# Splitting the first loads of a TensorE-bound LSTM and sign-weight FFN kernel into smaller pieces on two DMA queues

## The reference

```python
xW = einsum('ntd,dg->ntg', x, Wx) + b            # x (32, 64, 256), Wx (256, 1024)
for t in range(64):                               # LSTM, h and c (32, 256), h0 = cond
    a = xW[:, t] + h @ Wh                         # Wh (256, 1024)
    i, f, o, g = sigmoid(a0), sigmoid(a1), sigmoid(a2), tanh(a3)
    c = f * c + i * g
    h = o * tanh(c)                               # hs[:, t] = h
w0, w1, w2 = where(k0, 1, -1), where(k1, 1, -1), where(k2, 1, -1)
u = 2 * relu(s0 * (concat(hs, -hs) @ w0))         # 1024 features
u = 2 * relu(s1 * (u @ w1))                       # 1024
y = x + s2 * (u @ w2)                             # 256
```

## Time and profile before

| what | us |
|---|---|
| median of three runs | 278.2 |
| lowest and highest of them | 277.32 and 278.24 |
| the profiled execution, its own time | 277.77 |
| its span (first to last instruction) | 276.0 |
| TensorE busy in the span | 272.2 |

### The profile page before, as it was taken

The page is one execution under the profiler, slowest core; times in us unless marked ns, Lnnn a source line. Parts: engine busy times, 40 slices in busy tenths (PEclk is TensorE's granted clock), DMA queues, the critical chain, the costliest instruction groups (busy, mean ns, idle before and its releaser), DMA issues.

```text
span 276.0 us, 8792 instructions
## 1 busy us (share of the span) xinstructions
PE 272.2 (99%) x3616; PEld 224.0 (81%) x3616; DVE 203.5 (74%) x751; ACT 158.0 (57%) x482; POOL 2.2 (1%) x10
## 2 busy tenths in 40 slices
PE   8999999999999999999999999999999999999996
PEld 5887888888999998999999999999999996444443
DVE  3778888878888888888888888888887876532213
ACT  5689787878566656655555566555665554411100
POOL 0200000000000000000000000000000000000000
DMA  6970000000000000000000000000000000010002
GB/s 221 362 298 1 4 2 0 2 4 2 2 2 0 5 21 21 2 2 4 21 23 2 1 21 21 2 2 23 22 3 0 21 23 2 0 38 2 0 0 76
DMA packets 5191, 8.72 MB, mean 32 GB/s; under 512 B 672, under 2 KB 3488, under 8 KB 5024
## 3 DMA queue, kind: packets, MB, share of 16 engines
q1 hardware_dynamic: 4864, 7.64, 7.8%
q10 hardware_dynamic: 288, 0.52, 0.5%
HBM read 6.07 MB, written 2.10 MB: 30 GB/s over the span
## 4 chain that ended last, share of the span: by engine, by line
PE 97%; DMA 1%; DVE 0%; DVEq 0%; issue 0%
PE WK L465 50%; PE WK L448 14%; PE G L427 11%; PE ACC L481 10%; PE G L418 9%; DMA x<-in_x 1%; PE G L448 1%; PE ACC L448 1%; PE G L481 0%; DVE xs L715 0%; DVE x L662 0%; DVEq L237 0%
## 5 line engine op out<-in xcount | busy, mean ns | idle before, releaser
L465 PE MATMUL WK<-h,k 128*128 128x256 f16 (+1 forms) x992 | 124.2, 276 | 0.0
L465 PEld LDWEIGHTS WK<-h,k 128*128 128x128 fp8e5 x992 | 94.2, 98 | 13.4
L609 ACT ACTIVATE tT<-aT 128x128 f32<-128x128 f32 x126 | 39.0, 310 | 56.4 <-DVE aT L759 55.2
L655 DVE SCALAR_TENSOR_TENSOR h<-WK,h 128x256 f16<-128x256 f32 (+1 forms) x105 | 42.6, 439 | 24.7 <-ACT h L574 24.7
L759 DVE TENSOR_REDUCE aT<-G 128x128 f32<-128x256 f32 x128 | 48.1, 417 | 7.7 <-PE G L427 6.1
L574 ACT ACTIVATE h<-WK 128x256 f16<-128x256 f32 (+1 forms) x104 | 36.3, 387 | 28.8 <-PE WK L465 28.8
L556 ACT ACTIVATE G<-xw 128x256 f32<-128x256 f32 x126 | 46.6, 370 | 0.0
L448 PE MATMUL WK<-xs,wxs 128*128 128x512 f32 x168 | 42.5, 400 | 0.0
L427 PE MATMUL G<-h,w 128*128 128x64 f16 x1008 | 39.5, 192 | 0.0
L418 PEld LDWEIGHTS G<-h,w 128*128 128x128 f16 x1008 | 32.9, 96 | 5.8 <-DVE h L776 4.4
L448 PEld LDWEIGHTS WK<-xs,wxs 128*128 128x128 f32 x168 | 30.4, 188 | 5.9
(11 more groups left out here) (66 smaller groups left out, 132.8 us busy)
## 6 DMA issues: line engine op xcount, KB each, us to landing
x<-in_x SPq DMA_DIRECT2D x3, 512.0 KB, 7.8
out_y<-x SPq DMA_DIRECT2D x12, 128.0 KB, 1.8
xw<-in_wh SPq DMA_DIRECT2D x4, 256.0 KB, 4.8
k<-in_k SPq DMA_DIRECT2D x1, 1024.0 KB, 9.6
x<-in_x ACTq DMA_DIRECT2D x2, 256.0 KB, 3.8
xw<-in_wx SPq DMA_DIRECT2D x4, 128.0 KB, 3.9
xw<-in_wx SPq DMA_DIRECT2D x2, 256.0 KB, 5.1
k<-in_k SPq DMA_DIRECT2D x1, 512.0 KB, 6.9
```

The source lines that it names most:

```text
L465: ins = eng.matmul(layer_src(tile), w, rhs, start=a == 0, stop=last)
L609: eng.activation(tT[:, B * j0:B * j1], aT[:, j0:j1].rearrange("p j b -> p (j b)"), ACT.Tanh, scale=half_gain0 if t == 0 else half_gain).th ...
L655: eng.scalar_tensor_tensor(layer_dst(tile, 1), layer_src(tile), 0.0, layer_dst(tile, 0), ALU.max, ALU.subtract).then_inc(lo_made[tile[0]])
```

## The change

Wx's first piece (k=0, gate tiles 0-1, 128 KB) becomes two of 64 KB, one for each gate tile, so there are seven pieces. x's quarter 0, half k=0 is loaded in two DMAs of 128 KB: columns 0 to 255 by ACT's queue and columns 256 to 511 by SP's, behind the first piece of Wx. Its high part is made in two casts, the first columns by DVE and the last by ACT (`xh0_end`), and TensorE and `x_lo(0, 0)` wait for both. x's half k=1 moves from ACT's queue to SP's, behind Wx's third piece. In the first matmuls the order of (tile, a) changes so that tile 1's low-weight matmul comes after two more of tile 0's. `wx_hi` and `wx_lo` of the pieces are renumbered. Nothing is computed that was not computed before.

```diff
-WX_GROUPS = ((0, 1, 0, 2), (0, 1, 2, 4), (1, 2, 0, 2), (1, 2, 2, 4), (0, 2, 4, 6), (0, 2, 6, 8))
+WX_GROUPS = ((0, 1, 0, 1), (0, 1, 1, 2), (0, 1, 2, 4), (1, 2, 0, 2), (1, 2, 2, 4), (0, 2, 4, 6), (0, 2, 6, 8))
...
         def wait_x_hi(e, i, k):
             if i == 0 and k == 0:
                 e.wait_ge(xh0, 1)
+                e.wait_ge(xh0_end, 1)
...
-            for g in range(4):
-                load_wx(g)
+            load_wx(0)
+            eng.dma_start(x[:, 0, 0, 256:512], x_d[:, 0, 0, 256:512]).then_inc(dx0_end, 16)
+            load_wx(1)
+            load_wx(2)
+            eng.dma_start(x[:, 0, 1], x_d[:, 0, 1]).then_inc(dx0[1], 16)
+            load_wx(3)
+            load_wx(4)
             eng.dma_start(small[:, :], small_d[:, :]).then_inc(dsmall, 16)
             for g in range(4):
                 eng.dma_start(wh[:, 2 * g:2 * g + 2], wh_d[:, 2 * g:2 * g + 2]).then_inc(dwh[g], 16)
                 if g == 0:
-                    load_wx(4)
-            load_wx(5)
+                    load_wx(5)
+            load_wx(6)
...
             for a0 in (0, 3):
                 for j0 in (0, 2):
-                    for a in range(a0, a0 + 3):
-                        for j in (j0, j0 + 1):
-                            matmul(("x", 0, j), a)
+                    for j, a in ((0, 0), (1, 0), (0, 1), (0, 2), (1, 1), (1, 2)):
+                        matmul(("x", 0, j0 + j), a0 + a)
...
-            eng.dma_start(x[:, 0, 0], x_d[:, 0, 0]).then_inc(dx0[0], 16)
-            eng.dma_start(x[:, 0, 1], x_d[:, 0, 1]).then_inc(dx0[1], 16)
+            eng.dma_start(x[:, 0, 0, 0:256], x_d[:, 0, 0, 0:256]).then_inc(dx0[0], 16)
             e.wait_ge(zeroed, 1)
             eng.activation(warm[:, :], zero[:, 0:NJ], ACT.Tanh)
             wx_hi(0)
+            e.wait_ge(dx0_end, 16)
+            eng.activation(xs[:, 0, 0, 0, 256:512], x[:, 0, 0, 256:512], ACT.Copy).then_inc(xh0_end)
             wx_hi(1)
+            wx_hi(2)
             x_hi(0, 1)
-            wx_hi(2)
             wx_hi(3)
             wx_hi(4)
+            wx_hi(5)
             for j in range(4):
                 x_empty(("x", 0, j))
-            wx_hi(5)
+            wx_hi(6)
...
             e.wait_ge(dx0[0], 16)
-            eng.tensor_copy(xs[:, 0, 0, 0, :], x[:, 0, 0]).then_inc(xh0)
+            eng.tensor_copy(xs[:, 0, 0, 0, 0:256], x[:, 0, 0, 0:256]).then_inc(xh0)
             wx_lo(0)
             x_lo(0, 0)
             wx_lo(1)
+            wx_lo(2)
             x_lo(0, 1)
-            wx_lo(2)
             wx_lo(3)
+            wx_lo(4)
```

More of the change, by code:

```diff
@@ L309, in lstm_ffn @@
         dx0 = [sem(f"dx0_{k}") for k in range(2)]
+        dx0_end = sem("dx0_end")
         dx = [sem(f"dx{i}") for i in range(1, 4)]
@@ L314, in lstm_ffn @@
         wxh, wxl, whi, wlo, xh, xl = (sem(n) for n in ("wxh", "wxl", "whi", "wlo", "xh", "xl"))
-        xh0, xh1 = sem("xh0"), sem("xh1")
+        xh0, xh0_end, xh1 = sem("xh0"), sem("xh0_end"), sem("xh1")
         zeroed, maxed, max_all, scaled, biased, signed, hz_hi, hz_lo = (
@@ L727, in _ @@
                               apply_absolute_value=True).then_inc(maxed)
-            wx_lo(4)
+            wx_lo(5)
             for g in range(1, 4):
@@ L734, in _ @@
             eng.tensor_scalar(mx[:, 7:8], mx[:, 5:6], 2.0 ** -16, None, ALU.max).then_inc(maxed)
-            wx_lo(5)
+            wx_lo(6)
             e.wait_ge(max_all, 1)
```

## The result

The changed kernel takes 279.14 us (seven runs, 278.96 to 279.63) against 278.04 for the kernel before in the same comparison (seven runs, 277.21 to 278.34): ratio 1.0053, 95% interval 1.0039 to 1.0066. The medians differ by 1.1 us. The ratio says about 1.5 (1.1 to 1.8), since the seven times of the kernel before lie in two groups, 277.2 to 277.5 and 278.0 to 278.3, and their median is in the upper one. The kernel is slower, and the prediction (278.0, range 277.1 to 278.9) was wrong. The profiled execution took 279.63, span 277.8, so it is the slowest of the seven; the first experiment gives a more usual one.

What follows compares the result with a forecast made beforehand. TensorE, busy 272.2 of 276.0 us, was taken as the bound, its first matmul held by x's landing and cast. Profiled 277.77 less 0.2 for the earlier start, 0 elsewhere, gave 277.57, a median of 278.0 us; range 277.1 to 278.9.

Steps and rivals of the forecast that it cites:

- The rest of the front: Work after the first matmul starts, up to step 0: extra casts fit, and three more SP issues (1.36 us) cost nothing.
- the term put at 0 for the landings behind SP's queue: Wh and later loads, issued 1.36 us later, land no later, as they wait behind as many bytes as before: 0 us.
- The cover: Some 2 us of the 5.4 us flight of Wh's last piece, spent behind other bytes, was to absorb the later issue.
- the gain of 0.2 at the start: First matmuls on TensorE: starting 0.27 us earlier, at 4.50, keeps 0.12 to 0.27 us after the clock's rise; 0.2 taken.
- The second rival: Step 0 late: Wh's last piece lands 1.36 us later, less 0.49 slack, a loss of 0.87: 279.1 us; chance 0.07.
- The landing rule: First loads: a piece lands 0.84 us after the counter of bytes moved passes the bytes up to and including it.
- my floor of 4.4: First real matmul: the matmuls on zeros keep TensorE until about 4.4 us, so the start gains at most 0.4.
- The first rival: x's last columns land late on SP's queue, the first matmul starts at 5.35, 0.24 us lost: 278.4; chance 0.13.
- The third (small pieces): Two 64 KB Wx pieces take longer than one, cancelling the gain: 278.2 us; no change, by this or the clock, 0.25.
- the forecast's way: First matmuls: most of the earlier start is lost because they run at 1.2 GHz until the clock rises.
- the level rises at about 5.3: TensorE's clock goes from 1.2 to 2.4 GHz at about 5.3 us, after the change too.
- the rival of a late clock: TensorE's clock rises later, 0.34 us per matmul at the lower level: 279.6 us or above; chance 0.03.

Runs made afterwards that it cites:

- e1: The first experiment: the changed kernel run again without an edit; median 279.17 us, ratio 1.0053 to the kernel before.
- e13: Kernel before, with SP waiting for Wx's first piece to land before it issues `small` and all behind it; no DMA added; ratio 1.0037.
- e5: Kernel before plus three tiny DMAs on SP's queue, one behind each of Wx's first three pieces; 278.56 us against 277.60.
- e7: Changed kernel with Wx's last piece issued behind the sixth, ahead of three pieces of Wh; 279.57 us, ratio 1.0063.
- e2: Changed kernel with x's second half issued by ACT again, behind x's first columns; median 279.38 us, ratio 1.0060.
- e15: Kernel before with only x's first half in two loads (ACT and SP) and two casts; ratio 1.0081, five of six times 279.96 to 280.66.
- e3: Kernel before with only Wx's first piece split in two of 64 KB; ratio 1.0015.
- e18: e3 with `small` issued by ACT behind x; 277.84 us against 277.87 for the kernel before, ratio 1.0008.
- e9: Changed kernel with Wh in two loads instead of four and Wx's sixth piece ahead of them; ratio 1.0106, four of five times above 280.
- e11: The kernel before run again without an edit; 277.60 us, ratio 1.0001.
- e12: e9 with x's second half issued by ACT behind its first cast and tile 0's three matmuls first; ratio 1.0121 to the kernel before.
- e10: Kernel before with Wh in two loads instead of four and Wx's fifth piece ahead of them; ratio 1.0024.
- e8: Changed kernel with x's second half issued by ACT, in the code behind its table load and warm activation; median 279.20 us, ratio 1.0058.
- e16: Changed kernel with Wx's tile 1 and `small` issued by ACT behind x's first columns; ratio 1.0060 to the kernel before.
- e6: e2 with 20 matmuls on zeros in place of 16; median 278.86 us, ratio 1.0036 to the kernel before.
- e17: e15 with 20 matmuls on zeros in place of 16; ten runs 278.07 to 278.77 us, ratio 1.0024 to the kernel before.

## Why the prediction was wrong

*The step that failed* is in "The rest of the front", and it is the term put at 0 for the landings behind SP's queue: SP's three more issues were counted, 1.36 us in all, and then priced at 0, since Wh's last piece spends "some 2 us" waiting behind other bytes and the bytes are the same. That argument takes the DMA engines for full all the time. They are not when a queue is fed late: 139 to 158 GB/s from 3 to 4 us here. The cover was to be a shorter flight for a later issue. The last piece's flight grew instead, from 5.6 us before to 5.9 in e13, 6.2 in e5 and e1 and 6.9 in the first profile; issued 1.43 us later, it landed 2.05 and 2.74 us later (e1, first profile), and 0.70 and 0.88 us were lost ahead of gate tile 6. e13 shows the price of the issue time alone, 0.84 us; e5, 0.96.

*A second term failed*, the gain of 0.2 at the start. The 13th matmul was forecast at 7.67 and came at 8.49 in the first profile and 7.99 in e1, later than before (7.87). The changed kernel's second matmul started only 0.07 us (e1: 0.23) earlier than before, for want of Wx tile 1, and from there to the 13th the lower clock cost 0.69 us (e1: 0.35).

*The second rival was the right one, in part.* It priced exactly this, late landings from the three issues, at 0.87 us and 279.1, with a chance of 0.07; the time is 279.14. That the two numbers agree is luck: the slack that it took off belongs to step 0, and the losses at the start were not in it. It had TensorE wait at step 0, where the seeds end 0.6 us early before and 0.5 after the change. The wait is a stage earlier, at gate tile 6, for Wx's last piece, on the same queue behind Wh; I had not looked at its slack. e7 shows the two are coupled: moved ahead of Wh, the piece waits for DVE.

*The landing rule* (counter plus 0.84) was too coarse. It gave x's last columns 3.92, measured 1.17 + 2.4 = 3.6, and Wx tile 1 4.18, measured 1.65 + 3.2 = 4.9. So the first matmul came at 4.22, earlier than the 4.50 forecast and than my floor of 4.4, and the second only at 5.27. The first rival (x's end late) was wrong for the changed kernel and right for e2 and e15, where ACT's queue carried x's second half beside it. The third (small pieces) is open: with the split alone (e3) Wx's two tiles land at 3.40 and 4.19, where the whole piece landed at 3.98, and x's first half lands no later than before, but Wx's last piece is in flight for 6.1 us there and in e18, 0.5 longer than before. No wait of TensorE came of that.

*The clock.* The 0.55 us of the start are gone by the 13th matmul, as forecast in the main, but not by the forecast's way: the wait for tile 1 took them. That the level rises at about 5.3 was one sample. Five matmuls from 5.27 took 2.01 us in the changed kernel and five from 5.37 took 1.43 in e9; six from 4.78 took 1.63 in e11 and six from 4.23 took 2.89 in e12. The Trainium skill ("TensorE: Matmul & The Clock Gate", "The HAM clock gate") says the moment varies from run to run, and these rows agree. So the rival of a late clock was right too, in part: in the changed kernel's two profiles it cost 0.69 and 0.35 us, in e15's 2.1. How often it comes in the changed kernel's other runs isn't shown.

*What stays open.* Why loads take longer in flight from about 5 us on in every version whose front differs, e10 with fewer issues among them (7.5 us in flight for the last piece, 5.6 in e11). It is shown that a later issue is enough for a late landing (e13), not that it is needed: in e3, with one issue more, the engines moved only 146, 104 and 129 GB/s in the three windows from 6.0 to 7.5. No run takes the three issues off the changed kernel and leaves the rest; where the wait before tile 6 went (e2, e8, e16), another came. Why e12 and e9 lose 3 to 4 us in some runs was not profiled.

## What to carry over

Before pieces are split so that the first work starts sooner, count the issues they put ahead of everything behind them on the queue, and look up the slack of each later load, not of the last consumer alone: here three more issues cost 0.7 to 1 us, and the earlier start gave nothing by the 13th matmul. Don't price late issues at zero because the engines look full; see whether they are full in the windows in which the queue is refilled. On TensorE, an earlier start is worth little if the second matmul's weights aren't there, and a pause between the matmuls on zeros and the real ones can cost more than the start could bring.

## What the runs showed of the hardware

- After a pause of 0.7 us between the matmuls on zeros and the real ones TensorE stayed at 1.2 GHz for about twelve more matmuls in e15's profile, though not in e2's; four more matmuls on zeros removed the runs that took 1.5 to 2 us more (e6, e17). The moment of the rise moves without such a pause too: where TensorE didn't wait among them, the first six matmuls took between 1.63 us (e11) and 2.89 (e12).
- A DMA that ACT's code has behind a table load and an activation was issued 0.07 us after the load began, 1.2 us before the activation. Timeline of e8:

```profile
1.15 1.28 ACT L583 ACT_TABLE_LOAD   x1 [1.15 <-PEq L844]
1.22 0.40 ACTq L584 DMA_DIRECT2D x<-in_x  x1
```

- SP took 0.47 us from one issue to the next for a DMA of 256 bytes (e5, 1.17 to 1.64) and for one of 256 KB of Wh (before, 5.30 to 5.77). The 256 KB pieces of Wx took 0.60 and 0.66 (before, 5.77 to 6.37 and 3.53 to 4.19).
